# Graph kernel on one core: graph 1's count scatters with two groups of eight under way instead of one

## The reference

```python
src = jnp.concatenate([edge_index[0], loop])
dst = jnp.concatenate([edge_index[1], loop])
deg = jax.ops.segment_sum(jnp.ones_like(dst, dtype=XW.dtype), dst, num_segments=n)
dinv = jax.lax.rsqrt(jnp.maximum(deg, 1e-30))
norm = dinv[src] * dinv[dst]
msg = XW[src] * norm[:, None]
z_local = jax.ops.segment_sum(msg, dst, num_segments=n) + b_gcn
...
out = jax.nn.relu(z_local + z_global)
```

## Time and profile before

| | us |
|---|---|
| median of three runs (lowest, highest) | 6296.5 (6295.43, 6300.26) |
| the profiled execution, its own time | 6305.33 |
| its span | 6303.6 |
| POOL busy in it | 1604.4 (25%) |
| of this, graph 1's 416 scatters | 406.5, idle before them 402.3 |
| TensorE's matmuls busy | 4450.9 (71%) |
| DVE busy | 3123.4 (50%) |

### The profile page before, as it was taken

One profiled execution on the slowest core, in us unless ns is written; L12 is line 12 of the kernel. 1 busy time (PEld: TensorE's weight loads), 2 busy tenths in 40 slices (PEclk: granted clock), 3 DMA queues, 4 the chain that ended last, 5 costly groups with the idle time before them and its releaser, 6 DMA issues. The chain is left out here.

```text
span 6303.6 us, 60833 instructions
## 1 busy us (share of the span) xinstructions
PE 4450.9 (71%) x18528; PEld 2927.6 (46%) x18528; DVE 3123.4 (50%) x6025; ACT 2115.9 (34%) x4133; POOL 1604.4 (25%) x1750
## 2 busy tenths in 40 slices
PE   1230056995573867979995799996684867897898
PEld 1230044774010646757774123223574546574676
DVE  8441035113885538841114898985885026444211
ACT  5100001113573105622222687884562110203122
POOL 1466655664674531100000211100111010000000
PEclk9865578997786988979997898997896988898899
DMA  9300054115443535520001444441552327361000
GB/s 378 148 1 1 0 160 132 38 38 169 142 147 118 178 117 189 163 51 0 0 0 55 144 156 133 158 141 47 198 171 88 101 69 227 99 206 31 0 0 20
DMA packets 405633, 664.34 MB, mean 105 GB/s; under 512 B 108992, under 2 KB 210360, under 8 KB 399864
## 3 DMA queue, kind: packets, MB, share of 16 engines
q1 hardware_dynamic: 368152, 654.14, 31.4%
q0 software_dynamic: 37216, 7.08, 0.7%
HBM read 542.72 MB, written 118.31 MB: 105 GB/s over the span
## 5 line engine op out<-in xcount | busy, mean ns | idle before, releaser
L1195 PE MATMUL l2g_a_agg_acc<-all_x,l2g_a_h 128*65 128x512 f32 (+1 forms) x1400 | 653.8, 593 | 23.9 <-ACT l2g_a_agg_flat L1220 21.1
L385 POOL DMA_INDIRECT far<-all_nil,all_far_cell x416 | 499.1, 1200 | 313.2 <-DMA far<-all_nil,all_far_cell 150.4
L385 POOL DMA_INDIRECT table<-first_count,first_cell x416 | 406.5, 977 | 402.3 <-issue 279.9
L1293 DVE SCALAR_TENSOR_TENSOR all_x<-all_x,l2g_a_agg_counts 128x512 f32<-128x512 f32 (+1 forms) x700 | 405.1, 627 | 124.6 <-ACT all_x L1243 124.2
L853 PE MATMUL l0g_agg_acc<-l0g_agg_halves,l0g_agg_exact 128*128 128x512 f32 x625 | 154.9, 402 | 342.5 <-issue 340.4
L1232 ACT ACTIVATE l2g_a_agg_z<-l2g_a_agg_z 128x512 f32<-128x512 f32 (+1 forms) x700 | 344.3, 538 | 148.8 <-PE l2g_a_agg_z L1175 124.6
L853 PE MATMUL l3g_agg_acc<-l3g_agg_halves,l3g_agg_exact 128*128 128x512 f32 x1250 | 304.0, 398 | 90.3 <-DVE l3g_agg_exact L906 85.3
L1243 ACT ACTIVATE all_x<-l2g_a_agg_z 128x512 f32<-128x512 f32 (+1 forms) x700 | 353.4, 567 | 0.5 <-PE l2g_a_agg_z L1184 0.5
L1793 DVE SCALAR_TENSOR_TENSOR all_x<-l1f_moe_py,l1f_gate,all_x 128x256 f32 x200 | 96.8, 484 | 445.9 <-PE l1f_moe_py L1750 445.9
L1195 PEld LDWEIGHTS l2g_a_agg_acc<-all_x,l2g_a_h 128*65 128x65 f32 x1400 | 175.4, 148 | 287.0 <-issue 208.0
L853 PEld LDWEIGHTS l3g_agg_acc<-l3g_agg_halves,l3g_agg_exact 128*128 128x128 f32 x1250 | 236.9, 191 | 153.1 <-DVE l3g_agg_exact L906 86.2
(11 more groups left out here) (759 smaller groups left out, 9391.6 us busy)
## 6 DMA issues: line engine op xcount, KB each, us to landing
l3g_agg_counts<-table SPq DMA_DIRECT2D x250, 320.0 KB
l2g_a_agg_counts<-table SPq DMA_DIRECT2D x300, 256.0 KB
table<-counting_eye_rows SPq DMA_DIRECT2D x25, 1600.0 KB, 38.2
l0g_agg_counts<-table SPq DMA_DIRECT2D x125, 320.0 KB
l1g_agg_counts<-table SPq DMA_DIRECT2D x125, 320.0 KB
l2g_a_agg_mask<-far SPq DMA_DIRECT2D x50, 800.0 KB
l1g_gat_agg_counts<-table SPq DMA_DIRECT2D x150, 256.0 KB
l2g_b_agg_counts<-table SPq DMA_DIRECT2D x150, 256.0 KB
```

What stands on the lines that cost most here:

```text
L385: pool.indirect_dma_start(self.table, bass.IndirectOffsetOnAxis(ap=self.cell[:, b, p:p + 1], axis=0), self.count(b, p), None, bounds_check ...
L1195: pe.matmul(to, rhs(t, r * per + h), p[:, u % n_p, 0:n], start=(t == 0), stop=(t == nt - 1), skip_group_check=True).then_inc(summed, 1)
L1293: dve.scalar_tensor_tensor(out=w, in0=w, scalar=1.0, in1=counts[:, b % n_counts, 0:n], op0=ALU.min, op1=ALU.mult).then_inc(weighted, 1)
```

## The change

Graph 1's scatters get `open_windows` = 2 in place of 1. Graph 2's and the mask's keep 1.

```diff
-        scatter1 = Scatter(order1, table1, cell1, lambda b, p: count1[:, b, p:p + 1], landed[0], (table_set[0], 16 * T), 8, 1)
+        scatter1 = Scatter(order1, table1, cell1, lambda b, p: count1[:, b, p:p + 1], landed[0], (table_set[0], 16 * T), 8, 2)
```

## The result

The changed kernel took 6368.7 us in the median of four runs (6340.9 to 6378.7), the kernel before on the same chip 6296.0 (6290.2 to 6300.3). The ratio is 1.0109, with a 95% interval of 1.0076 to 1.0142: slower by 1.1%, where 6215 us had been forecast. The profiled execution took 6378.65 us on a span of 6376.9. The ratios in this document leave out two executions that lay far off all others of their kernel (9816.6 us of the wider pace and 6444.4 us of the kernel before, both in the fourth set).

The account below looks back on a forecast made before the run. POOL's scatters were taken to end the stages, other engines waiting at barriers, so its landing waits were kernel time. Savings of 56.8 and 24.7 us, others 0, sum to 81.5: 6296.5 - 81.5 = 6215.0 us, range 6202 to 6232.

Parts of the forecast that it names:

- A: Rival: graph 1's scatter queue is the slower side, waits return later, time stays near 6296 us; chance 3%.
- B: Rival: graph 1's scatters get dearer with two groups under way, 90 us more, time 6305 us; chance 2%.
- No stage changes its bound: POOL still ends every stage, its lead being 15.3 us in the layernorm, 15.1 in the Gram product, 327 in the second sort.
- rival C: Another engine takes over the stages; held excluded by the cover of 15 us and more, no chance of its own.
- 24.7 earlier: From 217 to 412.8 us, 15 landing waits of 29.2 us shrink to gaps of 0.302 us, saving 24.7 us.
- More transfers under way: 0: Graph 1's scatters, some three under way as before, cost nothing extra: 0, upper end 0.01 us per scatter, 4 us in all.
- equal waits behind two and behind eight: Around the barrier at 260 us, a 1.93 us wait behind two scatters and behind eight, taken as no queue backlog.
- a backlog would grow with the number: In POOL's scatter queue, a backlog would make the wait longer behind more scatters; it was 1.93 us either way.
- Behind the scatters everything moves forward as a block: Everything after 838.9 us shifts earlier unchanged, TensorE at the same clock: 0 extra, a few us either way.
- 56.8 us: From 412.8 us, in the second sort, 35 landing waits of 67.4 us shrink to gaps of 0.302 us, saving 56.8 us.
- 2.92 us wait: First stage's landing wait at j = 8: 0 saved, since SP issues until 217.2 us; upper end 2.6 us.
- 0.92 on one mechanism: Chance of 92% that removing graph 1's landing waits brings the forecast saving of 81.5 us.

Follow-up runs that it names:

- wider pace: Changed kernel with a clear of 256 bfloat16 elements on POOL ahead of each of graph 1's scatters: 6286.6 us, on another chip 6289.9 us.
- fourth set: On one chip, changed kernel 6373.6 us, wider pace 6289.9, groups of sixteen with one open 6247.7, of twenty-four 6277.7; kernel before 6297.9.
- The pause: Changed kernel with five POOL clears, some 27 us, ahead of graph 2's first scatter: 6236.8 us, on another chip 6273.6 us.
- the fours: Changed kernel with graph 2's scatters in groups of four, one open, instead of eight: 6314.0 us against 6292.5 of the kernel before.
- the two single runs: The changed kernel again, unchanged, in two separate runs: 6361.4 us against 6299.0 of the kernel before, and 6209.0 against 6284.6.
- the second set: On one chip, the pause 6236.8 us, early-only kernel 6266.5, wider pace 6286.6, groups of twenty-four with one open 6234.5; kernel before 6294.5.
- the last run: The changed kernel a fifth time, unchanged, on a chip with landing times: 6209.0 us against 6284.6 of the kernel before.
- early-only kernel: Changed kernel with two groups open for scatters 0 to 135 only, then one as before: 6266.5 us, on another chip 6290.6 us.

## Why the prediction was wrong

*The change itself* was read rightly. Landing waits are gone, scatters keep 0.97 to 0.99 us, and the idle time of the group fell from 402.3 to 346.1 us; what this is short of the 82 forecast are mostly new waits of POOL at barriers (ACTq L51 37.7 us in the group, 14.0 of them in the kernel before). Rivals A and B, backlog on the queue and dearer scatters, both stayed away in the sense I gave them: no landing wait came back, and the scatters cost 13 ns more in the mean, not 200.

*"No stage changes its bound"* failed, and with it the exclusion of rival C. The cover of 15 and 20 us that the other engines had was a cover for work at their old speed. In the crawl the layernorm's and the Gram product's stages end with the other engines' work, POOL waits 10.5 and 13.2 us for it, and the second sort begins 1.0 us later instead of 24.7 earlier.

*"More transfers under way: 0"* failed as an argument. The test I made, equal waits behind two and behind eight, looked at the landing alone. It cannot show what a scatter costs a path that others use: in groups of eight there is always a stop of 1.6 us behind, and the trace of before has no crawl. By theory R the sentence that a backlog would grow with the number was right and the backlog sat somewhere else than I looked; what the runs show is that with a mean pitch under 1.41 us the other engines' work slows down while POOL's own waits for landings stay short (nine in the aggregation, 1.94 us each). (The landing seen "at most 1.93 us" after the issue was misread too: the wait at 212.03 us took 2.92. With 8 us to spare this changed nothing.)

*"Behind the scatters everything moves forward as a block"* failed most dearly. The second sort's stage did give 47 of its 56.8 us, and its crawl is covered (DVE's last work at 687 us, POOL's last scatter at 787). But what it leaves behind met graph 2's scatters, at 1.48 us not far enough above the limit, and the aggregation's part of the time rose by 127 us (from 1031.08 - 846 to 1111.90 - 800, by POOL's and DVE's first work in the stages). The pause takes this away; the fours shorten it.

*On a chip without the crawl* the forecast held, by the mechanism that it named: 6209.0 us, in the range of 6202 to 6232, and 75.6 us under the kernel before where 81.5 were forecast. Step by step, trace against trace: the scatters behind the layernorm's stage begin at 255.56 instead of 263.34, 7.8 us less, of which the waits of that stage are the forecast 4.9. The rest is the first stage: I took its 2.92 us wait at 0 because SP's last issue ended at 217.2 us, but the next scatter comes at 218.94 instead of 221.86, so it was POOL that ended the stage, and the upper end of 2.6 us was the truth. Up to the second sort 27.9 us are gone (24.7 + 2.6 forecast), at POOL's last scatter 86.2, at the first matmul of the aggregation 86.2, at the stage behind it 81.8. The medians differ by some 6 us less; the two executions of this kernel on that chip, 6203.4 and 6214.6 us, lie further apart than that, so I don't ask where those went.

The chances were wrong in kind. All rivals spoke of this queue, this table and these waits, and 0.92 on one mechanism left no room for an effect that the trace of before does not hold, though the change took POOL out of the only pattern that the trace shows.

## What to carry to other kernels

A short wait on each group of small indirect transfers may guard nothing that is needed so soon, and still hold down the pace at which they pass something shared. Before taking it out, ask how long the engine has ever run without it in any trace, and take out half first (here sixteen in a group gained 44 and 50 us and twelve 30 on chips without landing times; on such chips the whole change lost 62 to 79). When a stage seems covered by another engine, look in the trace of the changed kernel at the spacing of its instructions, not only at their durations. And judge such a change on more than one chip: here one program was 1.0 to 1.2% slower in four sets of runs and 1.3% faster in a fifth, on another chip.

## What the runs showed of the hardware

- On the chips of five of the seven sets (the result's and the two single runs counted), scatters at a mean pitch under about 1.41 us (1.409 a little, 1.387 clearly; 1.417 not) slowed the other engines to a step of 0.70 us: DVE and TensorE instructions 0.7, 1.4 or 2.1 us apart with nothing to wait for, and late in the second sort POOL's moves 700 ns instead of 29. In the aggregation TensorE's count of finished blocks came five blocks late. On two chips (the kernels of the second set, and the last run) nothing of the kind happened at a pitch of 1.27 us.
- The kind of chip could be told from every trace kept here: where a kernel with a pitch under 1.41 us crawls, the list of DMA issues gives no landing time for graph 1's scatters (after: x416 and nothing behind it), not even for kernels that don't crawl, such as the kernel before; where none crawls, it gives 2.1 us. In the fourth set and the two single runs the sign and the crawl went together as expected. There is no trace of the kernel before on a chip that doesn't crawl; the early-only kernel and the wider pace, which don't crawl on either, show the sign on both. Without the crawl's trigger both kinds are about equally fast: the medians of the kernel before are 6289 to 6299 us on the one and 6285 to 6295 on the other, of the wider pace 6289.9 and 6286.6.
- Missing records and slow sequencers together look like a path for records that is slower on some chips and holds up those who write to it. The Trainium skill ("NOTIFIC — the notification-queue block", 7.1 Overflow: three behaviours, one of which stalls the engine) describes such a path, which stalls its producers rather than lose a record inside the block. No run here shows that this is the path: every timed execution came with its span and so was recorded, and whether an unrecorded one crawls on such a chip wasn't tried. It stays open, and with it whether the loss would be there outside a measurement.
- POOL's long clears hold DVE up: while five clears of 128x6400, 5.7 us each, ran beside the aggregation's first blocks, DVE's first five instances of L906 (there L913) took 3.6 to 5.5 us each, and 0.47 us once the clears were over. The mean of all 125 is 702 ns, 498 in the changed kernel.
